# A routed mixture-of-experts kernel: four buffers for the routing records, and rows gathered in quarters and transposed by VectorE

## The reference

```python
def reference(x, w_qkva, gamma, router_w, w0, w1, wo):      # x: [8, 1024, 256] float32
    x = x + attn(layernorm(x))       # rmsnorm, one projection to q, kv, a; scan y = sigmoid(a)*y + kv; q*y
    x = x + ffn(layernorm(x))
    return x

def ffn(h):                          # G = 8 groups of S = 1024 tokens, E = 8 experts
    logits = einsum('GSM,ME->GSE', h, router_w)
    # top 2 experts of each token with their gates; position of a token within its expert by a running
    # count over the group; capacity C = 256 of a group and expert, later tokens are dropped
    dispatch, combine = gating_top2(logits, C)
    xe = einsum('GSEC,GSM->EGCM', dispatch, h)
    hidden = gelu(einsum('EGCM,EMH->EGCH', xe, w0)) * einsum('EGCM,EMH->EGCH', xe, w1)   # H = 1368
    return einsum('EGCM,GSEC->GSM', einsum('EGCH,EHM->EGCM', hidden, wo), combine)
```

## Time and profile before

| | |
|---|---|
| median of 3 runs | 1694.92 us |
| lowest and highest | 1693.82 us, 1695.25 us |
| span of the profiled execution | 1694.7 us |
| TensorE busy | 1657.8 us, 98% |
| VectorE busy | 866.7 us, 51% |
| ScalarE busy | 723.9 us, 43% |
| GpSimd busy | 505.2 us, 30% |
| DMA mean | 57 GB/s |

### The profile page before, as it was taken

The page is one execution under the profiler, slowest core; times in us unless marked ns, Lnnn a source line. Parts: engine busy times, 40 slices in busy tenths (PEclk is TensorE's granted clock), DMA queues, the critical chain, the costliest instruction groups (busy, mean ns, idle before and its releaser), DMA issues.

```text
span 1694.7 us, 22843 instructions
## 1 busy us (share of the span) xinstructions
PE 1657.8 (98%) x8738; PEld 1435.3 (85%) x8738; DVE 866.7 (51%) x1827; ACT 723.9 (43%) x1325; POOL 505.2 (30%) x432
## 2 busy tenths in 40 slices
PE   8999979899999999999999999999999999999998
PEld 7888868788888888888888888888888888888887
DVE  7998744435544454346444644455445544464442
ACT  5776624234433443335333533344334433353332
POOL 2155556463222222222222222222222222222211
PEclk9999989999999999999999999999999999999999
DMA  7553121025111331124111511151114211241101
GB/s 165 160 157 115 52 77 53 3 43 127 33 26 26 91 61 26 26 53 92 20 26 23 121 21 26 26 118 33 26 26 94 58 26 26 56 90 20 23 11 15
DMA packets 124980, 96.21 MB, mean 57 GB/s; under 512 B 27144, under 2 KB 120776, under 8 KB 124872
## 3 DMA queue, kind: packets, MB, share of 16 engines
q1 hardware_dynamic: 96200, 60.66, 13.2%
q0 software_dynamic: 28672, 34.10, 12.1%
HBM read 60.11 MB, written 34.61 MB: 56 GB/s over the span
## 4 chain that ended last, share of the span: by engine, by line
PE 89%; POOL 3%; DVE 2%; DMA 2%; issue 2%; another core or an unknown queue 1%; ACT 0%; SPq 0%; POOLq 0%; DVEq 0%; ACTq 0%
PE bank L1579 27%; PE bank L1592 27%; PE bank L1608 17%; PE bank L1610 9%; PE bank L1396 4%; POOL slots L592 2%; PE bank L1482 2%; PE bank L1449 1%; DMA slots<-records,sloti 1%; PE bank L1603 1%; PE bank L1605 1%; POOL out L659 1%; PE bank L1437 1%; PE bank L1412 1%
## 5 line engine op out<-in xcount | busy, mean ns | idle before, releaser
L1335 DVE TENSOR_TENSOR y<-bank,sig 128x512 f32<-128x512 f32 (+1 forms) x352 | 243.0, 690 | 472.0 <-PE bank L1592 442.1
L659 POOL DMA_INDIRECT out<-xring,slot_records x128 | 214.7, 1678 | 890.7 <-DVE xring L1315 826.2
L1608 PE MATMUL bank<-wo,hhi 128*128 128x512 f32 (+1 forms) x1276 | 447.2, 388 | 0.0
L844 ACT ACTIVATE hhi<-y 128x512 fp32r<-128x512 f32 (+1 forms) x349 | 220.4, 631 | 524.5 <-DVE y L1335 486.7
L1610 PE MATMUL bank<-wo,hlo 128*128 128x256 f32 (+1 forms) x1396 | 382.0, 274 | 0.0
L1338 DVE TENSOR_TENSOR hlo<-y,hhi 128x512 fp32r<-128x512 f32 (+1 forms) x349 | 241.5, 692 | 243.4 <-ACT hhi L844 237.8
L834 ACT ACTIVATE sig<-bank 128x512 f32<-128x512 f32 (+1 forms) x352 | 208.9, 594 | 284.4 <-PE bank L1579 272.2
L1608 PEld LDWEIGHTS bank<-wo,hhi 128*128 128x128 f32 (+1 forms) x1276 | 239.2, 187 | 43.5
L1610 PEld LDWEIGHTS bank<-wo,hlo 128*128 128x128 f32 (+1 forms) x1396 | 261.7, 187 | 6.5
L1579 PE MATMUL bank<-xThi,whi 128*128 128x512 f32 x704 | 216.1, 388 | 7.0 <-ACT sig L834 5.4
L1592 PE MATMUL bank<-xThi,whi 128*128 128x512 f32 x704 | 213.0, 383 | 0.4 <-DVE y L1335 0.3
(11 more groups left out here) (134 smaller groups left out, 1571.0 us busy)
## 6 DMA issues: line engine op xcount, KB each, us to landing
stage<-in_L_ffn_w_kernel SPq DMA_DIRECT2D x160, 128.0 KB
stage<-in_L_ffn_wo_kernel SPq DMA_DIRECT2D x80, 128.0 KB
xring<-in_L_attn_x SPq DMA_DIRECT2D x16, 512.0 KB
out<-xring SPq DMA_DIRECT2D x16, 512.0 KB
x_rows<-rows SPq DMA_DIRECT2D x16, 512.0 KB
slots<-records,sloti POOLq DMA_INDIRECT x128
rows<-x_rows,slot_records POOLq DMA_INDIRECT x128
out<-xring,slot_records POOLq DMA_INDIRECT x128, 3.8
```

Of the source, the lines that this page charges most:

```text
L659: pool.indirect_dma_start(out_rows, bass.IndirectOffsetOnAxis(idx, 0), ysb[:, t % 2, j, :], None, compute_op=ALU.add).then_inc(added, 16)
L844: act.activation(h_high(e, t, hc)[0:n, :], hf[0:n, hc % 2, :], ACT.Copy).then_inc(h_hi, 1)
L1335: dve.tensor_tensor(hf[0:n, hc % 2, :], up_value(e, t, hc)[0:n, :], gel[0:n, hc % 2, :], ALU.mult).then_inc(mul_done, 1)
L1608: pe.matmul(lines(yb[j][:, :]), high, lines(wo[0:n, hc, :, :].rearrange("p s c -> p (s c)")), start=hc == 0, stop=end, skip_group_check=True)
```

## The change

There are two changes. **Records.** `records` and `sloti` get RING = 4 buffers by group modulo 4; a record now has one gate, token, source row and four piece numbers (`PIECE` + b = 4 × row + b), one record for each of a token's two copies, so `gates`, `gsel`, `gslot` and `expert_no` fall away and the gate is read from the record. Piece 5 of group g waits for the scatters of group g-4. GpSimd's set-up writes the constant columns with 20 more iotas for `records` in place of one, and 4 more for `fill`.

**Rows.** For experts 1 to 7 a row is gathered in four quarters of 64 numbers (`x2_pieces`), 16 indirect DMAs a tile in place of 4 (L660 of the new file), with indices from `piece_slots`, which SyncE loads with 4 DMAs of 32 partitions a tile (`load_pieces`, L519). `load_records` becomes 4 DMAs of 32 partitions (L508). VectorE transposes 32 × 32 blocks of the gathered quarters into `rowsT`, at chunks 4 and 6 (`TURN`) of the tile before (`turn_rows`, L1170), from SBUF to SBUF. `prepare` of experts 1 to 7 then has no TensorE part. The contraction index is spread differently over the partitions, and the weights of experts 1 to 7 are loaded in that order (`o (p k) h`) with as many descriptors. Expert 0 keeps the gather of whole rows and the transposes on TensorE.

```diff
+TURN = (4, 6)
@@ wait_scattered
-            if g.value >= 2:
-                eng.wait_ge(scattered[h][g.parity], SCATTERED * (g.value // 2))
+            if g.value >= RING:
+                eng.wait_ge(scattered[h][g.parity], SCATTERED * ((g.value - RING) // 2 + 1))
@@ load_records, and new load_pieces, on SyncE
-                sync.dma_start(slot_records[:, t], src.rearrange("o (p j) c -> p (o j) c", p=P)).then_inc(
-                    records_loaded[t], 16)
+                to = slot_records[:, t].rearrange("p j c -> p (j c)")
+                by_token = src.rearrange("o (i b j) c -> b i (o j c)", b=NB, j=FJ)
+                for b in range(NB):
+                    sync.dma_start(to[32 * b:32 * (b + 1), :], by_token[b]).then_inc(records_loaded[t], 16)
+
+            def load_pieces(n):
+
+                e, t, p = n // FT, n % FT, n % 2
+                if n >= FT + 2:
+                    sync.wait_ge(rows_loaded[p], landed_rows(n - 2))
+                at = (e * ESLOTS + t * T) * REC
+                flat = slots.rearrange("s c -> (s c)")
+                for b in range(NB):
+                    src = flat[at + b:at + b + 32 * NP * REC].rearrange("(i w) -> i w", i=32)
+                    sync.dma_start(piece_slots[32 * b:32 * (b + 1), p, 0:NP * REC - NB],
+                                   src[:, 0:NP * REC - NB]).then_inc(pieces_loaded[p], 16)
@@ expert, on SyncE
                         load_records(e + 1, t - 1)
+                    if FT <= FT * e + t + 3 < E * FT:
+                        load_pieces(FT * e + t + 3)
                     if t == FT - 1 and not last:
@@ gather, on GpSimd
+                pool.wait_ge(pieces_loaded[p], 16 * NB * ((n - FT) // 2 + 1))
+                into = rows2[:, p].rearrange("p j c -> p (j c)")
+                for i in range(NP):
+                    b, j = divmod(i, FJ)
+                    idx = piece_slots[:, p, i * REC + PIECE:i * REC + PIECE + 1].bitcast(I32)
+                    to = (j * NB + b) * PW
+                    pool.indirect_dma_start(into[:, to:to + PW], None, x2_pieces[t],
                                             bass.IndirectOffsetOnAxis(idx, 0)).then_inc(rows_loaded[p], 16)
@@ VectorE
+            def turn_rows(e, t, k):
+
+                n, p = FT * e + t, t % 2
+                dve.wait_ge(rows_loaded[p], landed_rows(n))
+                pieces = rows2[:, p].rearrange("p j c -> p (j c)").rearrange("p (n i k) -> p k n i", n=NP, k=KD)
+                dve.transpose(rowsT[:, k, :].rearrange("p (n i) -> p n i", n=NP), pieces[:, k]).then_inc(turned, 1)
@@ expert, on VectorE
-                        if hc == PREPARE[0] and t < FT - 1:
-                            gates(e, t + 1)
-                        elif hc == PREPARE[0] and not last:
-                            in_gate.begin(Turn(e), FT)
-                            in_gate.link(dve.tensor_scalar(expert_no[:, :], expert_no[:, :], 1.0, None, ALU.add))
-                            gates(e + 1, 0)
+                        if hc in TURN and FT <= FT * e + t + 1 < E * FT:
+                            turn_rows(*divmod(FT * e + t + 1, FT), TURN.index(hc))
@@ prepare, on TensorE
+                if e > 0:
+                    return
```

More of the change, by code:

```diff
@@ L52, in parity, with ring @@
         return self.value % 2
+    def ring(self, n):
+        return self.value % n
 def wait(eng, sem, turn, per, more):
@@ L97, in build @@
     REC = 8
-    GT1, GT2, EX1, TOK, SRC = range(5)
+    RING = 4
+    GATE, TOK, ROW, PIECE = range(4)
+    NB = P // 32
+    NP = T // 32
+    PW = D // NB
     ESLOTS = G * CAP
@@ L322, in build @@
         fx_lo = sem("fx_lo")
-        gate_done = sem("gate_done")
+        pieces_loaded = [sem(f"pieces_loaded{i}") for i in range(2)]
+        turned = sem("turned")
         part_done = sem("part_done")
@@ L387, in build, with landed_rows @@
         assert HC == 11
+        def landed_rows(n):
+            calls = [FJ if i < FT else NP for i in range(n % 2, n + 1, 2)]
+            return 16 * sum(calls)
         def staged(eng, e, hc):
@@ L1233, in step @@
                 if i.value == G - 1:
-                    gates(0, 0)
                     prepare(0, 0, 0)
```

93 lines of the change are left out of this document (49 added, 44 removed).

## The result

The first comparison gave 1895.76 us (median of 4 runs, 1886.44 to 1901.44) against 1694.37 for the kernel before: a ratio of 1.119, with a 95% interval of 1.116 to 1.122. The forecast was 1691 us, so it was wrong by 205 us. The experiments then showed that one number isn't enough.

| kernel, session | this, us | before, us | ratio, 95% |
|---|---|---|---|
| changed, first session | 1895.8 | 1694.4 | 1.119 [1.116, 1.122] |
| changed, third session | 1696.0 | 1685.1 | 1.006 [1.005, 1.008] |
| changed, fourth session | 1934.6 | 1698.9 | 1.140 [1.135, 1.144] |

A forecast was written before the change was run, and what follows sets the result against it. TensorE, busy 98% of the span, was taken to bound the kernel. From the profiled 1694.7 us, - 25 - 4.7 + 19.2 + 6.7 gave 1690.9, forecast as 1691 us, range 1667 to 1702.

The forecast's parts named there:

- Transposes off TensorE: TensorE in 28 tiles: 56 groups of transposes at 0.44 us leave the path, 25 us gained; VectorE's replacements hide.
- Four record buffers: Routing: VectorE's waits for scatters go, but GpSimd's power is late next; 4.7 us gained, bounds 0 and 11.5.
- Sixteen gathers ahead of tile 2's additions: Expert 0: additions, then expert 1's weights come late; TensorE stalls 16.1 us plus 3.1 for clock, 19.2 lost.
- The rival that the gathers go at the additions' pace: GpSimd ahead of tile 2's additions: 16 gathers take 31.7 us in place of 21.2, total 1701 us; chance 0.15.
- SyncE's small DMAs in the other experts: Experts 1 to 6: 2.5 us of small DMAs ahead of weights, 1.1 us lost each, 6.7 in all; ends 0 and 12.6.
- a rival on the gain's side: Routing: TensorE's 5.4 us wait after ScalarE's unnamed gap moves, or GpSimd's queue moves up 4.52 us; about 1682 us, chance 0.13.

The follow-up runs named there:

- calm sessions: Second, third and sixth sets of comparisons run together on one chip, profiles without unexplained idle stretches of ScalarE and VectorE in the experts; kernel before takes 1685 us.
- Before with 16 gathers and no small loads: Kernel before plus 12 unread gathers of 256-byte pieces a tile in experts 1 to 7; 1703.13 us, ratio 1.011, later 1961.6 us, ratio 1.156.
- the weights first and the loads merged: Changed kernel, first four weight chunks ahead of small loads, one DMA each for a tile's records and pieces, one wait behind gather eight; 1655.07 us, ratio 0.982.
- four buffers alone: Kernel before with four buffers for records and slots, nothing else changed; 1678.97 us, ratio 0.9965, and again 1678.84 us, ratio 0.996.
- gappy session: First, fourth or fifth set of comparisons, profiles with ScalarE and VectorE idle over 2.4 us without a recorded releaser; kernel before takes 1694 to 1699 us.
- weights first: Changed kernel, but SyncE issues the next expert's first four weight chunks ahead of the small loads; 1947.27 us, ratio 1.147.
- with waits: Changed kernel with the first four weight chunks ahead of small loads and GpSimd waiting for landing after every fourth gather; 1679.26 us, ratio 0.989.
- whole rows: Changed kernel with four gathers of whole rows a tile in experts 1 to 7 instead of 16 of quarters, small DMAs kept; 1695.87 us, ratio 1.006.

## Why the prediction was wrong, point by point

**Transposes off TensorE, -25: right.** A VectorE transpose of 128x512 takes 0.70 us against 0.69 assumed, and no wait for one is listed. A tile of the experts takes 43.93 us against 44.86 (from the first addition of one tile to that of the next, calm sessions): 28 × 0.93 = 26 us.

**Four record buffers, -4.7: right.** -6.1 us alone. Piece 5 of `place` no longer waits for scatters, and VectorE's longest wait for GpSimd's power is 5.7 us at the factors (L1034, session 3), which is what was said to be late next.

**Sixteen gathers ahead of tile 2's additions, +19.2: right in a calm session.** TensorE stands 16.95 us (16.1 forecast) and comes back at 0.50, some 5 us long (the earlier trace rows had 6.2); with the same 3.1 us for the clock that makes 20.1. Before with 16 gathers and no small loads shows the same by itself: 1703 against 1685. The rival that the gathers go at the additions' pace, 1.98 us, did not come: they go at 1.013 + 0.30.

**SyncE's small DMAs in the other experts, +6.7: less than half of what they cost.** From the first addition of one tile to that of the next, the six tiles with an expert's change in them take 278.5 us together in session 3, and 263.3 with the weights first and the loads merged: 15.2 us more. A small DMA takes 0.43 to 0.46 us, not 0.36, and each weight DMA behind them 0.60, not 0.47, a cost of the new order that was not costed. TensorE waits 1.8 to 2.4 us in place of the 1.1 forecast, 11.8 in all; the clock fell to 0.50 behind one of these six waits only. This lies above the upper end that the prediction gave, 12.6.

**The routing's loads of records: a term that was missing.** The first additions of expert 0 start 7.5 us later than with four buffers alone (347.82 against 340.37). With the loads merged they start at 342.26, so 5.6 us of it are the four loads in place of one; the rest isn't settled. The prediction counted SyncE's extra DMAs only ahead of weights. `load_records(0, 0)` stands ahead of a load of `x` that VectorE waits for.

By these, a calm session makes 26 + 6.1 - 20.1 - 15.2 - 7.5, a loss of 10.7 us; the runs say 11. That they agree so well is in part luck: the term of 20.1 is partly an estimate, and the changed kernel ends 12.6 us after its last tile's additions begin, the kernel before 11.1, which no term holds.

**The step that failed** is none of the four terms. It is the sentence "In experts 1 to 6 GpSimd has room (it idles 890.7 us ahead of additions, and 28 × 12 more gathers at 1.325 us are 445), so only the 2.5 us count". It takes a run of 16 indirect DMAs to cost its own issue time and nothing else. In two sessions of three in which the changed kernel ran, ScalarE and VectorE were held up behind such runs for 2.6 to 11 us at a time, and the first of them cost 190 us in all against the calm session (spans 1884.5 against 1694.1), 4.5 of it before the first additions of expert 0 and some 6.6 in each of 28 tiles. The evidence was in the trace of before, in small: ScalarE's unexplained gap behind such a run, which the prediction booked as a rival on the gain's side and never asked what would make more of them. As a rival it had the wrong sign.

**What stays open.** Why one session is gappy and another calm: the same binaries did both, and so did the chip numbered 8. How ScalarE and VectorE are held: GpSimd's own pace, 1.0 us in the mean + 0.30, is the same in both kinds, TensorE was seen to wait only for the others, and no row names a releaser. That a run of gathers issued without a wait brings the gaps on in a gappy session is shown by 1961.6 against 1698.0 in session 5, where 12 unread gathers a tile are the only difference. That waits alone take them away rests on two gappy sessions: weights first took 1947.3 in session 4, and with waits 1679.3 in session 5. At which length it begins isn't shown. A rival that nothing here rules out is the recording: every run listed here was recorded with its span and clock, the gappy traces lack from a fifth to over a half of the DMAs' events, and a run of 16 gathers makes many of them at once. If the recording holds the engines, a run without it would not show the gaps.

## What to carry to other kernels

Count not only how many DMAs an engine issues but how many it issues in a row without a wait for their landing. Where a profile has idle stretches that nothing releases, list them with what GpSimd was doing ahead of them before adding more of the same, and leave out those that are plain waits; a wait for landing after every fourth cost 4 to 7 us here in calm sessions, and with it the gaps of the experts were gone in a gappy one. Take more than one session before a difference is believed: a loss of 200 us was there in two and not in the third. And a queue in which bulk loads stand behind small ones is as late as the small ones are many: put the loads that a tuned pipeline waits for first, and price each small DMA at what the queue shows for it, every place of the queue included, not only the one in view.

## What the runs showed of the hardware that had not been expected

- The same binary took 1696 us in one session and 1896 or 1935 in others, with each session's own runs within 0.8%. The kernel before moved by under 1% between them (1685, 1694, 1699), so its times alone hardly gave the state away. The gappy sessions' traces also lack events of the DMAs, 8942 against 20405 for the changed kernel. The Trainium skill ("DMA: Bandwidth & Descriptors", SWDGE vs HWDGE vs iDMA) says that GpSimd writes the descriptors of such DMAs into rings itself. As a cost on GpSimd that does not show here: its gathers take 1.000 us in the mean in the first session and 1.013 in the third, while ScalarE's and VectorE's idle stretches differ.
- A wait of TensorE for `y` of 3.0 to 3.4 us was followed by the granted clock at 0.50 in all six cases (whole rows, session 2), one of 1.8 to 2.4 us in one of six (changed kernel, session 3).
- With the new row order of the `w` loads, their issue on SyncE's queue took 0.60 us each in place of 0.47, and so did that of the `wo` load between them, whose own pattern hadn't changed.
- A gather's issue took 1.0 us in the mean + 0.30 for 256-byte pieces as for 1 KB rows (1.025), in runs of 16 too, and the VectorE transpose of 128x512 0.70 us, where the estimate from the Trainium skill ("VectorE: DVE Perf Modes", the three transpose paths) had been 1.2.
